# First cross attention: scores in two turns of two banks, transposes of 64-row tiles in pairs, the output weight one tile later, the context behind the difference

## The reference, cut to what matters

```python
x = x + _L0_attn_ref(...)                      # gated linear attention
x = x + _L0_xattn_ref(_layernorm(x), ctx, ctx, in_proj_weight, in_proj_bias, out_w, out_b)
x = x + _L0_ffn_ref(...)                       # small attention and mixture of experts
# ... second layer
```

## Time and profile before

| | us |
|---|---|
| median of 3 runs (438.1 to 438.87) | 438.15 |
| the profiled execution | 440.88 |
| its span in the trace | 438.8 |
| TensorE busy / ScalarE busy / VectorE busy, whole span | 404.4 / 295.5 / 347.3 |
| mean granted TensorE clock, as a share of full speed | 0.973 |

### The profile page before, as it was taken

The page is one execution under the profiler, slowest core; times in us unless marked ns, Lnnn a source line. Parts: engine busy times, 40 slices in busy tenths (PEclk is TensorE's granted clock), DMA queues, the critical chain, the costliest instruction groups (busy, mean ns, idle before and its releaser), DMA issues.

```text
span 438.8 us, 14149 instructions
## 1 busy us (share of the span) xinstructions
PE 404.4 (92%) x5148; PEld 300.4 (68%) x5148; DVE 347.3 (79%) x944; ACT 295.5 (67%) x720; POOL 218.1 (50%) x558
## 2 busy tenths in 40 slices
PE   8999978997878999769999999999999998989887
PEld 6465646775865777536777777777777776878647
DVE  4798969675769998968888888888888886566785
ACT  3774534775458788248888888889898885432540
POOL 7470011570221557515787878877787886520100
PEclk9999988999899999989999999999999999998998
DMA  7299975600000131000000000000000000000001
GB/s 234 68 98 100 99 80 171 201 17 2 1 0 13 50 108 32 19 1 3 19 5 19 4 19 3 19 3 1 1 3 1 4 2 3 3 1 1 0 1 48
DMA packets 15635, 16.03 MB, mean 37 GB/s; under 512 B 1348, under 2 KB 12859, under 8 KB 15579
## 3 DMA queue, kind: packets, MB, share of 16 engines
q1 hardware_dynamic: 15579, 15.24, 17.0%
HBM read 10.52 MB, written 4.72 MB: 35 GB/s over the span
## 4 chain that ended last, share of the span: by engine, by line
PE 68%; DVE 17%; ACT 6%; POOL 4%; issue 3%; DMA 1%; SPq 0%; DVEq 0%; POOLq 0%; ACTq 0%
PE bank L1526 11%; PE bank L1477 9%; PE bank L1444 7%; PE bank L1394 5%; PE bank L992 4%; PE bank L1313 4%; PE bank L1300 3%; PE bank L1200 3%; PE bank L1388 2%; PE bank L1518 2%; PE bank L1664 2%; PE bank L1410 2%; PE bank L1094 2%; DVE Y L1694 1%; DVE amxs L2240 1%
## 5 line engine op out<-in xcount | busy, mean ns | idle before, releaser
L898 ACT ACTIVATE SN<-SN,nmx 128x512 f32<-128x512 f32 x128 | 91.4, 718 | 0.0
L2062 DVE CUSTOM_DVE_ANT_0 SN<-bank,strip 128x512 f32<-128x512 f32 x128 | 82.8, 684 | 0.3 <-issue 0.2
L1477 PE MATMUL bank<-TK,TQ 64*128 64x512 f16 x384 | 53.2, 383 | 2.1 <-DVE TK L2029 2.1
L1444 PEld LDWEIGHTS bank<-cs,SN 64*128 64x128 f32 x1024 | 42.3, 140 | 12.5 <-issue 0.7
L1444 PE MATMUL bank<-cs,SN 64*128 64x64 f32 x1024 | 42.6, 224 | 0.0
L569 POOL TENSOR_TENSOR CTW<-YT 128x128 f32<-128x128 f32 x64 | 29.6, 463 | 14.9 <-ACT YT L911 11.9
L1526 PE MATMUL bank<-Z,TV 128*64 128x128 f32 x512 | 33.4, 273 | 0.0
L1526 PE MATMUL bank<-PTO,TV 128*64 128x128 f32 x512 | 33.3, 273 | 0.0
L997 PE MATMUL bank<-ones 128*128 128x128 f32 x220 | 32.0, 301 | 1.0 <-POOL konst L405 1.0
L573 POOL TENSOR_TENSOR CTX<-CTW,CTX 128x128 f32 (+1 forms) x64 | 27.4, 428 | 10.5 <-POOL CTX L571 9.2
L997 PEld LDWEIGHTS bank<-ones 128*128 128x128 f32 x220 | 29.9, 214 | 3.5 <-issue 2.2
(11 more groups left out here) (331 smaller groups left out, 977.7 us busy)
## 6 DMA issues: line engine op xcount, KB each, us to landing
bias_rows<-biasr SPq DMA_DIRECT2D x1, 4096.0 KB, 45.2
band<-bias_rows SPq DMA_DIRECT2D x1, 3072.0 KB, 11.4
wqkv<-in_twqkv SPq DMA_DIRECT2D x8, 192.0 KB, 2.9
w1s<-in_w SPq DMA_DIRECT2D x8, 128.0 KB, 2.6
w2s<-in_w SPq DMA_DIRECT2D x8, 128.0 KB, 2.5
wB<-in_wb SPq DMA_DIRECT2D x1, 753.0 KB, 6.2
wA<-in_wa SPq DMA_DIRECT2D x1, 520.0 KB, 4.9
X<-in_x SPq DMA_DIRECT2D x2, 256.0 KB, 3.1
```

The costliest lines, as they stand in the source:

```text
L898: sc.activation(p, p, ACT.Exp, bias=nmx[:, r % RING, h:h + 1], scale=-1.0, accum_out=psm[:, r % RING, h:h + 1]).then_inc(sm["exp_ready"], 1)
L1444: ins = nc.tensor.transpose(bank[4 + half][:, c:c + TD], SN[q, r % RING, h, P * kt:P * kt + P], ident[q, q])
L1477: ins = mm(bank[2 * (s % 2) + h][:, :], TQ[u][r, q_part, S * b + P * qt:S * b + P * qt + P], TK[u][r, k_part, S * b:S * b + S], start=(k = ...
L2062: vv.tensor_tensor_reduce(out=SN[:, r1 % RING, h, :], in0=bank[2 * (r1 % 2) + h][:, :], in1=strip[u1][:, h, c1:c1 + S], scale=-1.0, scalar ...
```

## The change

`KX` gets a copy for each of two turns, masked to 4 of the 8 heads that lie in a half of 64 rows. `xs(i, turn)` makes the scores of turn 0 in banks 0 and 1 (j = 0 and 2) and of turn 1 in banks 2 and 3 (j = 1 and 3), with 64-row matmuls, one for each half. VectorE reduces and subtracts each turn by itself, and ScalarE takes the Exp of each turn by itself. The 12 transposes become 24 of 64 rows: the lower half of the rows goes to bank 4, the upper one to bank 5. The first two pieces are made together for all j, the third one later. `ctx_o` works in four 32-column matmuls, and a tile later than before. `ctx_norm(i-2)` comes behind the difference. `residual(0)` moves to the last round of the loop, and ScalarE's `rstd_of(3, 0)` behind the last copy. The scores of tile i+2 stand ahead of the last piece's transposes.

```diff
 def expand_keys(part):
-                m = inside[:, :].rearrange(...)
-                gp.tensor_tensor(KX[:, part, :, :, :], k, m, ALU.mult)
+                for turn in range(2):
+                    m = halves[:, HG * turn:HG * turn + HG].rearrange(...)
+                    gp.tensor_tensor(KX[:, turn, part, :, :, :], k, m, ALU.mult)
...
+            exponential_of(0, 0)
             for i in range(NT):
-                act.wait_ge(sm["px_sub"], i + 1)
-                sc.activation(PX[:, i % 2, :, :], PX[:, i % 2, :, :], ACT.Exp, scale=XD ** -0.5)
+                exponential_of(i, 1)
                 if i >= 1:
                     inverse_sums(i - 1)
+                if i == 1:
+                    take_yt(1, 1)
+                take_first_pieces(i, 0)
+                if i == 0:
+                    rstd_of(1, 1)
+                take_first_pieces(i, 1)
+                if i == 1:
+                    query_high(1)
+                if i + 1 < NT:
+                    exponential_of(i + 1, 0)
+                take_last_piece(i)
                 if i == NT - 1:
                     rstd_of(3, 0)
-                if i == 1:
-                    take_yt(1, 1)
-                for c, (_, n) in enumerate(PIECES):
-                    ...
-                    sc.copy(PT[0:n, i % 2, c, :], bank[4 + c % 2][0:n, :])
...
-            def xs(i):
+            def xs(i, turn):
...
-                    pe.wait_ge(sm["px_sub"], i)
+                    pe.wait_ge(sm["px_sub"], 2 * i - 1 + turn)
                 for k, (q_part, k_part) in enumerate(PRODUCTS):
-                    for j in range(XH // HG):
-                        r = slice(HR * j, HR * j + HR)
-                        ins = mm(bank[j][:, 0:GN], QT[r, ...], KX[r, k_part, ...])
+                    for half in range(2):
+                        r = slice(P // 2 * half, P // 2 * half + P // 2)
+                        ins = mm(bank[2 * turn + half][:, 0:GN], QT[r, ...], KX[r, turn, k_part, ...])
...
+                for q in range(P // HR):
+                    r = slice(HR * q, HR * q + HR)
+                    ins = mm(bank[7][r, ...], CT[:, i % 2, r], wB_("out", P), start=True, stop=True)
...
+            def first_pieces(i):
+                for turn in range(2):
+                    pe.wait_ge(sm["px_ready"], 2 * i + turn + 1)
+                    for j in (turn, turn + 2):
+                        for c in range(2):
+                            for half in range(2):
+                                ins = turned_piece(i, c, j, half)
+                ins.then_inc(sm["pt_mm"], 2)
...
             for i in range(NT):
                 if i == 1:
                     norm_half(1, Y, 1)
-                pe.wait_ge(sm["px_ready"], i + 1)
                 if i >= 1:
                     pe.wait_ge(sm["pt_ready"], 3 * i)
-                piece_t(i, 0)
-                piece_t(i, 1)
+                first_pieces(i)
                 if i == 1:
                     queries(1)
-                    pe.wait_ge(sm["ct_ready"], 1)
+                if i + 2 < NT:
+                    for turn in range(2):
+                        xs(i + 2, turn)
+                pe.wait_ge(sm["pt_ready"], 3 * i + 2)
+                last_piece(i)
                 if i == 2:
                     pe.wait_ge(sm["qt_ready"], 2)
-                    ctx_o(0)
                 if i >= 2:
-                    ctx_o(i - 1)
+                    ctx_o(i - 2)
                 if i == 0:
                     pe.wait_ge(sm["x_done"], 2)
-                pe.wait_ge(sm["pt_ready"], 3 * i + 1)
-                piece_t(i, 2)
+                else:
+                    pe.wait_ge(sm["ct_ready"], i)
                 for c in range(len(PIECES)):
-                    if c == 2 and i + 2 < NT:
-                        xs(i + 2)
-                    pe.wait_ge(sm["pt_ready"], 3 * i + c + 1)
+                    if c == 2:
+                        pe.wait_ge(sm["pt_ready"], 3 * i + 3)
                     times_values(i, c, 0, values)
...
+            ctx_o(NT - 2)
             ctx_o(NT - 1)
...
 def subtract_max(i):
+                for turn in range(2):
+                    dve.wait_ge(sm["s_mm"], 2 * i + turn + 1)
+                    ins = vv.tensor_reduce(in_turn(mx3, turn), s4[:, 2 * turn:2 * turn + 2], AX.X, ALU.max)
+                link(ins)
                 if i >= 2:
                     dve.wait_ge(sm["pt_mm"], 3 * (i - 1))
-                dve.wait_ge(sm["s_mm"], i + 1)
-                link(vv.tensor_reduce(mx, s4, AX.X, ALU.max))
+                for turn in range(2):
+                    vv.tensor_tensor(in_turn(px4, turn), s4[:, 2 * turn:2 * turn + 2], m, ALU.subtract).then_inc(sm["px_sub"], 1)
                 if i >= 2:
                     ctx_norm(i - 2)
-                ins = vv.tensor_tensor(PX, s4, m, ALU.subtract)
...
                 if i == NT - 1:
-                    dve.wait_ge(sm["x_done"], 3)
-                    norm_stats(2, 0, X)
-                if i == TG + 1:
                     dve.wait_ge(sm["co_mm"], TG)
                     dve.wait_ge(sm["xb_ready"], 1)
                     residual(0, XB, 7, 1)
+                    dve.wait_ge(sm["x_done"], 3)
+                    norm_stats(2, 0, X)
```

More of the change, by code:

```diff
@@ L765, in inverse_sums, with exponential_of, take_first_pieces @@
                 sc.activation(rc[:, :], rc[:, :], ACT.Exp, scale=-1.0).then_inc(sm["rc_ready"], 1)
+            def exponential_of(i, turn):
+                act.wait_ge(sm["px_sub"], 2 * i + turn + 1)
+                px = in_turn(PX[:, i % 2, :, :].rearrange("p (j h) s -> p j h s", h=HG), turn)
+                sc.activation(px, px, ACT.Exp, scale=XD ** -0.5).then_inc(sm["px_ready"], 1)
+            def take_first_pieces(i, half):
+                n = PIECES[0][1]
+                act.wait_ge(sm["pt_mm"], 3 * i + 2)
+                if i >= 2:
+                    act.wait_ge(sm["xo_mm"], i - 1)
+                dst = PT[0:n, i % 2, 0:2, :].rearrange("p c (j h q) -> p c j h q", h=2, q=P // 2)[:, :, :, half, :]
+                sc.copy(dst, bank[4 + half][0:n, :].rearrange("p (c j q) -> p c j q", c=2, q=P // 2)).then_inc(sm["pt_ready"], 1)
@@ L767, in _, with take_last_piece @@
+            def take_last_piece(i):
+                n = PIECES[2][1]
+                act.wait_ge(sm["pt_mm"], 3 * i + 3)
+                dst = PT[0:n, i % 2, 2, :].rearrange("p (j h q) -> p h j q", h=2, q=P // 2)
+                sc.copy(dst, banks[0:n, 4:6, 0:2 * P].rearrange("p h (j q) -> p h j q", q=P // 2)).then_inc(sm["pt_ready"], 1)
+            exponential_of(0, 0)
             for i in range(NT):
-                act.wait_ge(sm["px_sub"], i + 1)
-                sc.activation(PX[:, i % 2, :, :], PX[:, i % 2, :, :], ACT.Exp, scale=XD ** -0.5).then_inc(sm["px_ready"], 1)
+                exponential_of(i, 1)
@@ L1185, in ctx_o, with turned_piece, last_piece @@
                     pe.wait_ge(sm["x_done"], 2 + 1)
-                mm(bank[7][:, P * (i % TG):P * (i % TG) + P], CT[:, i % 2, :], wB_("out", P), start=True, stop=True).then_inc(sm["co_mm"], 1)
-            def piece_t(i, c):
-                a, n = PIECES[c]
-                px = PX[:, i % 2, :, :].rearrange("p h s -> p (h s)")
+                for q in range(P // HR):
+                    r = slice(HR * q, HR * q + HR)
+                    ins = mm(bank[7][r, P * (i % TG):P * (i % TG) + P], CT[:, i % 2, r], wB_("out", P), start=True, stop=True)
+                ins.then_inc(sm["co_mm"], 1)
+            def turned_piece(i, c, j, half):
+                a, n = PIECES[c]
+                q = slice(P // 2 * half, P // 2 * half + P // 2)
+                px = PX[q, i % 2, HG * j:HG * j + HG, :].rearrange("p h s -> p (h s)")
+                at = 2 * P * (c % 2) + P // 2 * j
+                return nc.tensor.transpose(bank[4 + half][0:n, at:at + P // 2], px[:, a:a + n], ident[q, q])
+            def first_pieces(i):
[6 more added lines that the diff above has]
+                ins.then_inc(sm["pt_mm"], 2)
+            def last_piece(i):
                 for j in range(XH // HG):
-                    ins = tr(bank[4 + c % 2][0:n, P * j:P * j + P], px[:, GN * j + a:GN * j + a + n])
+                    for half in range(2):
+                        ins = turned_piece(i, 2, j, half)
                 ins.then_inc(sm["pt_mm"], 1)
@@ L1207, in _ @@
             gla_t(1)
-            xs(0)
+            for turn in range(2):
+                xs(0, turn)
             gla_out(1)
-            xs(1)
+            for turn in range(2):
+                xs(1, turn)
             for i in range(NT):
@@ L2286, in nth_norm, with in_turn @@
     return 5 + 2 * g + 3 - n if n in (2, 3) else 2 * n + g + 1
+def in_turn(a, turn):
+    return a[:, turn:XH // HG:2]
 def where(r):
```

38 lines of the change are left out of this document (14 added, 24 removed).

## The result

The time of the changed kernel is 442.94 us (median of 20 runs, 439.31 to 451.09), beside 439.41 for the kernel before (20 runs, 435.93 to 447.27): ratio 1.0087, 95% interval 1.0066 to 1.0109, some 3.8 us more. (The ratios leave out the slow runs, of which the kernel before had more, and so the medians lie only 3.5 apart.) The forecast was 438.6, that is 0.4 more, with a range up to 440.0. So it was slower, by far more than the forecast and than rival 1 (439.3). It is about what rival 3 had (441.9, which is 3.8 over 438.15), but, as will be seen, not for rival 3's reason.

What follows compares the result with a forecast made beforehand. Two limits bound a tile: the path through reciprocal and context (4.14 us) and TensorE's work (about 4.05). Start +1.25, five tiles -0.62, end -0.21 sum to +0.4 on 438.15, so 438.6 us; own range 437.4 to 439.2, full 437.1 to 440.0.

Steps and rivals of the forecast that it cites:

- rival 1: Tile 0: a longer TensorE gap brings the clock down before tile 2's scores; +0.7 us, 439.3; chance 0.28.
- rival 3: Paired 64-row transposes don't pay: 70 ns each, TensorE 4.49 us a tile, near 441.9; chance 0.07 in full or part.
- What bounded the kernel before: Middle tile: path through reciprocal and context 4.14 us, TensorE's own work about 4.05; taking one away alone brings next to nothing.
- TensorE's work, the transposes: Each tile: 24 transposes of 64 rows at the later stage's 31 ns, 0.74 us, where twelve took 1.56.
- The bounds: Price of one 64-row transpose: 31 ns as in the later stage, up to 70 ns if pairs don't overlap (1.68 us).
- The path of a tile: Middle tile: reciprocal, copies, half Exp, last copy, last values and sums through ScalarE; 3.93 us, 0.38 above TensorE's sum.
- Five tiles: From tile 2's sums to tile 7's: 20.27 us before, 5 x 3.93 = 19.65 after; gain 0.62.
- The start: Tiles 0 and 1: tile 0's sums 1.05 later, piece transposes -0.3, way through ScalarE +0.49; in all +1.25 us.
- VectorE's halves: Reduction and difference each made in two halves; in tile 0, tile 1's difference ends 0.15 us later.
- the queries' way through ScalarE: Tile 1, end of queries to end of sums: 3.01 us through ScalarE where 2.52 before, 0.49 more.
- The clock: Profiled execution taken to stand 2.7 us above the median in both kernels, so 441.3 profiled gives a median of 438.6.
- The end: Behind tile 7 only the output weight changes, from 0.49 to 0.28 us: -0.21.

Runs made afterwards that it cites:

- e12: Kernel before (103 columns) with the output weight a tile later and residual(0) in the last round, context still ahead of the difference; ratio 1.0046.
- e16: Kernel before with 104/104/100 pieces, output weight a tile later, context ahead of the difference, residual(0) after tile 6's difference; ratio 0.9995.
- e7: Kernel before with only the piece width changed, to 104/104/100 columns; ratio 0.999.
- e3: Changed kernel with only the piece width changed, to 104/104/100 columns; one run, 437.34 us.
- e6: Changed kernel with only the piece width changed, to 104/104/100 columns, now with times; ratio 1.0034.
- e5: Changed kernel with 104/104/100 pieces and, in tile 0, tile 2's scores back behind the first two pieces' values; ratio 1.0021.
- e14: e5 with the output weight moved ahead of the wait for the copies and the last piece's transposes; ratio 1.005.
- e8: Changed kernel with five products of ones filling TensorE's gap in tile 0 ahead of tile 2's scores; ratio 1.0025.
- e4: Changed kernel with one order changed: in tile 0 alone, tile 2's scores back behind the first two pieces' values; ratio 1.0041.
- e1: Changed kernel with only the piece width changed, to 128/128/52 columns; ratio 1.0092.
- e2: Kernel before with only the piece width changed, to 128/128/52 columns; ratio 1.0044.
- e15: Changed kernel run again, unchanged; ratio to the kernel before 1.0084.

## Why the prediction was wrong, by its own steps

**What bounded the kernel before.** Right in one half: cutting the path through the context alone brings the tile only to 4.06 (e12; 4.05 in e16). The other half, that less work for TensorE alone leaves it at 4.14, is not shown, since e7 made the transposes only 0.04 us cheaper.

**TensorE's work, the transposes.** The step that failed most in the tiles: 31 ns from the earlier trace rows was taken for "same 64 rows, same 64 moving columns". Measured 55 ns for 103 columns (0.89 for 16), 38 for 104, 41 for 128. I left out two things: the stationary width (0.23 us of 16 transposes; the loads of L992 in the trace of before already had it) and how the group begins behind the sums (0.17). The bounds (31 to 70 ns) held. Rival 3 took its price from the upper one and got 0.07; its 441.9 is the measured size by luck, as it has tiles of 4.49 where 4.23 was measured, and nothing of the clock.

**The path of a tile.** The size 3.93 was right for 104 columns (3.95 in e3, e6, e5, e14), the list incomplete: the ring over both engines. By the forecast's own terms it would have been 0.49 + 1.07 + 0.25 + 0.28 + 1.63 = 3.72, below ScalarE's; measured it is 0.60 + 1.10 + 0.43 + 0.36 + 1.41 = 3.90 with 104 columns and 4.19 with 103, and 0.04 of hand-overs. So the mechanism, ScalarE's copies on the path in place of the context, was met, and the mis-sized term is the transposes: 0.28 of the 0.30 us between 3.93 and 4.23 go with the width (3.95 in e3). Rival 3's sign, a TensorE busy throughout, was not met.

**Five tiles.** From tile 2's sums to tile 7's after takes, by its timeline, 107.27 - 86.10 = 21.17 against 20.27: +0.9 instead of -0.62. Tile 2 itself, taken as even, has 4.23 in e8 against 4.17 in e7.

**The start.** Sign and mechanism right, size too small. With full clock on both sides, from the first scores to the end of tile 1's sums, e7 takes 78.58 - 63.77 = 14.81 and e8 80.73 - 64.06 = 16.67: +1.86, where 1.25 was forecast. Of that tile 0 has 11.22 against 9.89, +1.33 (forecast 1.05). The mis-sized term is VectorE's halves: the difference ends 8.62 us behind the start of the first scores against 8.26, +0.36 where 0.15 was taken; what stands behind it costs 0.97, near the 0.90 forecast. Tile 1 has +0.53 (forecast 0.19): the queries' way through ScalarE is there, but the transposes, at 55 ns each, gave little back. e4 shows which edit it is, the order in tile 0.

**The clock.** The error was in the profile that I took for both kernels. Its loop holds 2.85 us of low clock, and I carried its distance from the median, 2.7 us, over to the changed kernel; the profile of after stands 0.6 under its median (442.33 against 442.94), with about as much low clock as the rest of its runs (0.973 against a mean of 0.975). The stretch of low clock at 75.5 is in the one profile of before, and in none of the eight other profiles with the old tile 0 in that place; of ten with the changed kernel's transposes nine have one that begins between 70 and 77, and the tenth is the filled e8. So it was no common cost. Rival 1 (0.28) had the place nearly right. Its price of 0.7 was too low because it stood against a baseline that already paid: measured 1.1 to 1.2. Its reason, the longer gap, has e8 for it, but e4, e5 and e14 have tile 0's old order, with a gap of 1.64 us in e4, and fall as well.

**The end.** 0.49 became 0.43, -0.06 instead of -0.21.

**The sum.** Start 1.86, tile 2 0.06, tiles 0.9, clock 1.15, end -0.06: 3.9 us against the measured 3.8. The loop's own length says the same: 43.26 and 43.16 against 39.26 and 39.78. The agreement is better than the evidence: the terms come from single profiles, and stretches of low clock behind the loop differ from profile to profile too (10.2 us from 110 in after, 3.4 in e15). What is not settled is how the parts add in the time: e4, e6 and e8, each undoing one of them, all land at 1.0025 to 1.0041, and e5 with two at 1.0021, with intervals of ±0.003 to 0.004; the profiles of e5, e6 and e14 have a low stretch of 6.8 us where the others have 3.4.

## What to carry to other kernels

A price per instruction carries over from another stage only with all three sizes, the stationary width too, and with the same kind of product ahead of it; read the weight load's own row and the distance between starts beside the matmul's. When a width is changed, look at what becomes of the last, narrow piece. When a path is cut, list every ring that is left, also those that cross two engines twice, before taking the longest. And a low clock in one profile is one draw: before it is put on both sides of a sum, see in what order of work it comes back.

## What the runs showed of the hardware

- A weight load of 103 f32 columns, for a transpose of 64 or 128 rows, took 166 to 169 ns (before, after), of 100, 102 or 104 columns 122 to 133 (before, after, e3, e7), of 128 columns 138 (after, later stage).
- Transposes of 64 rows in pairs started 91 ns from pair to pair with 103 stationary columns (after), 56 with 104 (e3), 63 with 128 (e1). Transposes of 128 rows started 109 ns apart with 103, 104 and 128 columns alike (before, e7, e2).
- Where a product with 128 contraction rows was followed by one with 52, or the other way round, the next record started 200 ns after the last one instead of 88 to 90 (e1); from the sums to the 64-row transposes it was 200 as well (after, e3, e1).
- Filling 1.4 us of a TensorE gap of 2.8 us with products went with a granted clock of 1.00 where the unfilled kernel fell to 0.50 (e8 against after and e15, one profile each), worth 1.1 to 1.2 us of the loop.
